# Sixteen heads of a batch in one PSUM bank, and the maxima turned in the other

## The reference

```
sc = silu(c); shift = sc @ shift_w.T + shift_b
scale = clip(sc @ scale_w.T + scale_b + 1, 0.1, 10)
adaln(x) = x / max(rms(x), 1e-6) * norm_w * scale + shift
q, k, v = heads of adaln(x) @ qkv_w.T
p = softmax(where(mask, q k^T / sqrt(8), -inf))
x = x + (p v) @ proj_w.T + proj_b
h1, h2 = split(adaln(x) @ w1.T + b1)
out = x + silu(h1) * h2 @ w2.T + b2
```

## Time and profile before

| | us |
|---|---|
| median of 3 runs | 184.35 |
| lowest, highest | 181.88, 184.48 |
| profiled execution, whole | 180.74 |
| its span in the profile | 178.8 |
| busy: PE, DVE, ACT, POOL | 146.9, 141.4, 134.7, 83.1 |

### The profile page before, as it was taken

One profiled execution on the slowest core, in us unless ns is written; L12 is line 12 of the kernel. 1 busy time (PEld: TensorE's weight loads), 2 busy tenths in 40 slices (PEclk: granted clock), 3 DMA queues, 4 the chain that ended last, 5 costly groups with the idle time before them and its releaser, 6 DMA issues.

```text
span 178.8 us, 3725 instructions
## 1 busy us (share of the span) xinstructions
PE 146.9 (82%) x1312; PEld 75.7 (42%) x1312; DVE 141.4 (79%) x248; ACT 134.7 (75%) x245; POOL 83.1 (46%) x133
## 2 busy tenths in 40 slices
PE   7778776668898889879769879788889976998992
PEld 7564233413333333333233333332225854785870
DVE  8756895978999999977999977996253947987992
ACT  8469862195897888958879958899877799599550
POOL 8319508965923304734618733335200525544650
PEclk9879999999999999999999999999999999999999
DMA  4847461537403375422022122022140300010103
GB/s 111 253 161 208 137 168 42 149 84 205 127 15 108 108 210 149 150 89 92 2 89 70 32 95 83 6 90 91 43 126 8 109 12 0 2 59 0 59 4 117
DMA packets 17512, 16.38 MB, mean 92 GB/s; under 512 B 2846, under 2 KB 16598, under 8 KB 17494
## 3 DMA queue, kind: packets, MB, share of 16 engines
q1 hardware_dynamic: 16086, 15.21, 27.6%
q0 software_dynamic: 1408, 0.93, 2.0%
HBM read 4.34 MB, written 5.24 MB: 54 GB/s over the span
## 4 chain that ended last, share of the span: by engine, by line
DVE 35%; PE 29%; issue 15%; ACT 10%; POOL 8%; DMA 2%; DVEq 0%; POOLq 0%; ACTq 0%
DVE neg_max L1107 24%; ACT p_exp L959 5%; POOL gated_lo L509 5%; PE bank L679 5%; PE bank L609 5%; PE bank L661 2%; DMA q_stack<-max_rows 2%; PE bank L635 2%; PE bank L630 2%; PE bank L564 2%; PE bank L728 2%; PE bank L529 1%; PE bank L553 1%; DVE rest L1082 1%; DVE k_stack L1017 1%
## 5 line engine op out<-in xcount | busy, mean ns | idle before, releaser
L1107 DVE TENSOR_REDUCE neg_max<-bank 128x2 f32<-128x512 f32 x128 | 81.5, 686 | 9.2 <-PE bank L609 8.8
L959 ACT ACTIVATE p_exp<-bank 128x512 f32<-128x512 f32 x128 | 69.8, 603 | 15.7 <-PE bank L661 14.6
L679 PE MATMUL bank<-p_exp,v_all 128*9 128x256 f32 x512 | 39.5, 381 | 0.3
L609 PE MATMUL bank<-k_stack,q_stack 62*128 62x256 bf16 x256 | 25.2, 271 | 17.2 <-DVE neg_max L1107 14.0
L509 POOL TENSOR_TENSOR gated_lo<-rs,gated_hi 128x512 fp32r<-128x512 f32 x14 | 18.2, 1302 | 28.8 <-ACT gated_hi L981 27.6
L473 POOL DMA_DIRECT2D q_stack<-max_rows x32 | 17.7, 556 | 22.7 <-DVE max_rows L1116 22.7
L661 PE MATMUL bank<-q_stack,k_stack 64*128 64x256 bf16 x256 | 25.3, 270 | 3.6 <-ACT p_exp L959 3.0
L609 PEld LDWEIGHTS bank<-k_stack,q_stack 62*128 62x128 bf16 x256 | 8.9, 93 | 43.4 <-DVE neg_max L1107 38.7
L463 POOL CAST max_parts<-neg_max 128x16 bf16<-128x16 f32 x16 | 3.1, 195 | 29.5 <-DVE neg_max L1107 29.5
L661 PEld LDWEIGHTS bank<-q_stack,k_stack 64*128 64x128 bf16 x256 | 12.2, 94 | 10.3 <-ACT p_exp L959 4.8
L728 PE MATMUL bank<-h_hi,w_parts 128*128 128x512 f32 x32 | 13.0, 407 | 1.6 <-DVE rs L1233 1.4
(11 more groups left out here) (115 smaller groups left out, 217.5 us busy)
## 6 DMA issues: line engine op xcount, KB each, us to landing
o_rows<-o_sb SPq DMA_DIRECT2D x16, 256.0 KB, 2.1
q_stack<-parts SPq DMA_DIRECT2D x18, 128.0 KB
k_stack<-parts SPq DMA_DIRECT2D x18, 128.0 KB
o_num<-o_rows SPq DMA_DIRECT2D x8, 128.0 KB, 2.4
o_den<-o_rows SPq DMA_DIRECT2D x8, 128.0 KB, 3.2
out_t<-o_num SPq DMA_DIRECT2D x8, 128.0 KB, 2.0
back<-back_w SPq DMA_DIRECT2D x1, 832.0 KB, 8.2
x_sb<-x_t SPq DMA_DIRECT2D x3, 256.0 KB, 4.9
```

Source lines behind the costliest of these rows:

```text
L609: mm = nc.tensor.matmul(scores[r][:, t * N:(t + 1) * N], q_stack[rows, c % STACKS, g, at + t * 128:at + (t + 1) * 128], k_stack[rows, c % ...
L679: mm = nc.tensor.matmul(bank[32 * j:32 * j + VW, 6 + k % 2, (q % 2) * N:(q % 2 + 1) * N], v_all[:, b, t, 2 * g + j, :], p_exp[:, (2 * q + ...
L959: nc.scalar.activation(p_exp[:, u % 4, par, :, :], bank[:, RING + v % RING, :].rearrange("p (t q) -> p t q", t=KT), ACT.Exp, scale=D ** -0 ...
L1107: nc.vector.tensor_reduce(out=neg_max[:, k % 2, :, par, g], in_=bank[:, n % RING, :].rearrange("p (t k) -> p t k", t=KT), axis=AX.X, op=AL ...
```

## The change

**One bank to a batch.** All 16 heads of a batch go into one bank, 6 for even batches and 7 for odd. Four quads of heads: quads 0 and 1 on rows 32j to 32j+8 (left and right half), quads 2 and 3 on rows 32j+16 to 32j+24. For that every head's piece of `v_all` is 25 columns wide, 8 values, a one and 16 zeros, and every stationary has 25 columns: for quads 0 and 1 it begins at the head's values, for quads 2 and 3 16 columns earlier, in the zeros of the head before. Quads add up in the bank; only the batch's first matmuls start it. ACT drains a bank once per batch (batches 0 to 5), DVE batches 6 and 7; one store and two loads per batch. `proj_w`'s rows are put in the new order on the host.

**Turns in the idle bank.** From k = 2 on the turned maxima go into bank 6 or 7, whichever the next batch will use, and no longer into the ring; they have semaphores of their own (`s_turn`, `s_turned`). The mean squares of chunks 0 and 1 go into bank 6 (`s_squares`). The first P times V of a batch waits for the copy of the second turn in its bank, the even turns wait for the drain of the batch before last.

**Constants.** POOL fills 16 zeros behind each head's one; `valid` shares memory with the mask to make room.

```diff
 RING = 3
+RING_TURNS = 2
...
-        items += [("turn", k) for k in range(HALVES) if turn_position(k) == p]
+        items += [("turn", k) for k in range(RING_TURNS) if turn_position(k) == p]
         items += [("project", c) for c in range(NC - 1) if project_position(c) == p]
-        items += [("square", c) for c in range(NC - 1) if square_position(c) == p]
+        items += [("square", c) for c in range(EARLY, NC - 1) if square_position(c) == p]
...
+def turn_bank(k):
+
+    return 6 + k // 2 % 2
+
+
+def square_bank(c):
+
+    return 6 + (BC * (c + 1)) % 2
...
-        v_all = sb("v_all", [C, B, KT, H, VW])
+        v_all = sb("v_all", [C, B, KT, H, V_WINDOW])
...
-            nc.gpsimd.memset(v_all[:, :, :, :, D:VW], 1.0).then_inc(s_const, 1)
+            heads = v_all.rearrange("p b t h w -> p (b t h) w")
+            nc.gpsimd.memset(heads[:, :, D:VW], 1.0).then_inc(s_const, 1)
+            nc.gpsimd.memset(heads[:, :, VW:V_WINDOW], 0.0).then_inc(s_const, 1)
...
             def turn_maxima(k):
-                turned = ring_bank(item("turn", k))
+                if k < RING_TURNS:
+                    turned, done = ring_bank(item("turn", k)), s_a
+                else:
+                    turned, done = bank[:, turn_bank(k), :], s_turn
+                    if k % 2 == 0 and k >= 4:
+                        pe.wait_ge(s_od, k // 2 - 1)
+                    if k % 2:
+                        pe.wait_ge(s_turned, k - RING_TURNS)
+                    for c in range(EARLY):
+                        if k == 4 * (c + 1) + 5:
+                            pe.wait_ge(s_inv2, 2 * c + 1)
                 pe.wait_ge(s_mp, 2 * (k + 1))
...
             def mean_square_2(c):
-                squares = ring_bank(item("square", c))
+                if c < EARLY:
+                    squares, done = bank[:, square_bank(c), :], s_squares
+                    pe.wait_ge(s_turned, 4 * (c + 1) + 4 - RING_TURNS + 1)
+                else:
+                    squares, done = ring_bank(item("square", c)), s_a
...
-                b, g = divmod(2 * q, G)
-                k = q // 2
+                b, quad = divmod(q, 4)
+                side, half = divmod(quad, 2)
                 if t == 0:
                     pe.wait_ge(s_e, 4 * q + 4)
...
-                    if q % 2 == 0 and k >= 2:
-                        pe.wait_ge(s_od, k - 1)
+                    if quad == 0 and b >= 1:
+                        pe.wait_ge(s_turned, 2 * b + 1 - RING_TURNS + 1)
                 for j in range(4):
-                    mm = nc.tensor.matmul(bank[32 * j:32 * j + VW, 6 + k % 2, (q % 2) * N:(q % 2 + 1) * N],
-                                          v_all[:, b, t, 2 * g + j, :],
+                    first = (4 * quad + j) * V_WINDOW - side * V_AT
+                    mm = nc.tensor.matmul(bank[32 * j:32 * j + V_WINDOW, 6 + b % 2, half * N:(half + 1) * N],
+                                          v_all[:, b, t, :, :].rearrange("p h w -> p (h w)")[:, first:first + V_WINDOW],
                                           p_exp[:, (2 * q + j // 2) % 4, j % 2, t, :],
-                                          start=(t == 0), stop=(t == KT - 1), tile_position=(0, 32 * j))
+                                          start=(quad == 0 and t == 0), stop=(quad == 3 and t == KT - 1),
+                                          tile_position=(0, 32 * j))
...
-                if u % 4 == 2 and 6 <= u < UNITS - 2:
-                    drain_output(u // 4 - 1)
+                if u % G == LAG and G < u < G * (B - 1):
+                    drain_output(u // G - 1)
...
-                if p == UNITS - 2 + LEAD:
-                    drain_output(HALVES - 2)
+                if p == G * (B - 1) + LAG + LEAD:
+                    drain_output(B - 2)
```

More of the change, by code:

```diff
@@ L26 @@
 VW = D + 1
+V_AT = 16
+V_WINDOW = V_AT + VW
 EPS = 1e-6
@@ L141, in drained @@
 def drained(n):
-    return sum(not (what[0] == "square" and what[1] < EARLY) for what in ITEMS[:n + 1])
+    return n + 1
+def turn_bank(k):
+    return 6 + k // 2 % 2
+def square_bank(c):
+    return 6 + (BC * (c + 1)) % 2
 def build(nc, x_t, small, mask, front_w, back_w, out_t):
-    o_rows = nc.dram_tensor("o_rows", [B, H, 32, N], F32).ap()
+    o_rows = nc.dram_tensor("o_rows", [B, 2, 4, 32, N], F32).ap()
     ctx = ExitStack()
@@ L378, in _ @@
                     stacks_of(e, j)
-            for k in range(HALVES):
-                if k == 3:
+            for b in range(B):
+                if b == BC - 1:
                     stacks_of(NP - 1, 0)
[L382 to L385, removed]
+                store_outputs(b)
+                load_outputs(b)
+                if b == BC - 1:
                     stacks_of(NP - 1, 1)
@@ L466, in _ @@
                                         ALU.subtract).then_inc(s_mp, 1)
-                pool.wait_ge(s_ad, drained(item("turn", k)))
+                pool.wait_ge(*((s_ad, drained(item("turn", k))) if k < RING_TURNS else (s_turned, k - RING_TURNS + 1)))
                 c, at = divmod(k // 2, BC)
@@ L586, in ring_bank @@
                 if n >= RING:
-                    if ITEMS[n - RING][0] == "square" and ITEMS[n - RING][1] < EARLY:
-                        pe.wait_ge(s_inv2, 2 * ITEMS[n - RING][1] + 1)
-                    else:
-                        pe.wait_ge(s_ad, drained(n - RING))
+                    pe.wait_ge(s_ad, drained(n - RING))
                 return bank[:, n % RING, :]
@@ L632, in mean_square_2 @@
             def mean_square_2(c):
[L633 removed]
+                if c < EARLY:
[3 more added lines that the diff above has]
+                    squares, done = ring_bank(item("square", c)), s_a
                 pe.wait_ge(s_sq2, c + 1)
[L635 removed]
+                nc.tensor.matmul(squares, mean_w[:, :], sq2[:, c % 2, :], start=True, stop=True).then_inc(done, 1)
             def zero_outputs():
@@ L920, in square_2 @@
                 act.wait_ge(s_y3, 1)
-                act.wait_ge(s_a, item("square", c - 2) + 1)
+                act.wait_ge(s_squares, c - 2 + 1)
                 nc.scalar.activation(sq2[:, c % 2, :], y[:, c, :], ACT.Square).then_inc(s_sq2, 1)
@@ L925, in ln_norm_2 @@
                 if c < EARLY:
-                    n = item("square", c)
-                    act.wait_ge(s_a, n + 1)
-                    nc.scalar.activation(rs2[:, c, :], bank[:, n % RING, :], ACT.Ln, bias=words[:, 2:3]).then_inc(s_inv2, 1)
+                    act.wait_ge(s_squares, c + 1)
+                    nc.scalar.activation(rs2[:, c, :], bank[:, square_bank(c), :], ACT.Ln,
+                                         bias=words[:, 2:3]).then_inc(s_inv2, 1)
                     return
@@ L1263, in turned @@
         return np.ascontiguousarray(np.asarray(a).T)
+    by_output = [(m % 2) * C // 2 + (m // 2) * D + d for m in range(H) for d in range(D)]
     by_row = [(2 * g + r) * D + d for r in range(2) for d in range(D) for g in range(G)]
```

67 lines of the change are left out of this document (36 added, 31 removed).

## The result

| | before | changed |
|---|---|---|
| median, us (20 runs each) | 183.8 | 186.11 |
| lowest | 181.0 | 184.1 |
| profiled execution, whole | 180.74 | 188.29 |
| its span | 178.8 | 186.5 |

The ratio is 1.0192, with a 95% interval of 1.0154 to 1.0229: slower, by about 2%. The forecast of 180.6 us was wrong in sign, and 186.11 lies outside its range.

What follows compares the result with a forecast made beforehand. The prediction took the middle as bound by DVE's maxima waiting for PE's scores behind turned maxima in the three-bank ring. It summed 3.9 - 0.3 - 0.4 + 0.47 - 0.3 = 3.4 us gained, forecasting 180.6 us, range 177.0 to 183.6.

Steps and rivals of the forecast that it cites:

- the zeros in `v_all`: At the start: POOL's extra memset takes 3.6 us while POOL is idle, costing nothing; upper bound 2.1 us.
- rival 4: At the start: POOL's zeros come late by up to 2.1 us; 1.3 gained, 183.1 us. Chance 0.08.
- The turns, 9 x 0.43: Middle: turned maxima out of the ring save 0.43 us at k = 4-7, 9-11, 13, 14; 3.9 us together.
- Turns 2, 3, 8 and 12: Middle: k = 3 is late anyway; 2 waits for the maxima's DMA, 8 and 12 for POOL's square; 0 gained.
- rival 1: Middle: the DMA of the turned maxima becomes the bound; 1.5 us gained, 182.8 us. Chance 0.20.
- The 0.3 taken off for k = 4: At k = 4: the turn can't come sooner, so it gives 0.12 us, not 0.43; minus 0.3.
- The wider loads: P times V: 25 columns instead of 9 cost 0.04 us a group; 0.4 on the turns' path, 0.3 in the tail.
- rival 3: PE becomes the bound through loads at 0.11 us a group; 0.9 us lost, 185.3 us. Chance 0.10.
- The tail, +0.47 for a copy of ACT: From 120 us on: one drain per batch removes ACT's copy at 122.03 from the deciding path; 0.47 us gained.

Runs made afterwards that it cites:

- e2: The kernel before, with only v_all widened to 25 columns and its zeros set at the start; stationaries stay at 9 columns. 186.89 us, ratio 1.0195.
- e9: The changed kernel with half of the zeros set at the start and the other half behind the first K stacks. 185.88 us, ratio 1.0183.
- e5: Second run of e1's kernel: the changed kernel with POOL's memset of the zeros moved behind the first K stacks' DMAs. 181.43 us, ratio 0.993.
- e10: e8 with POOL's last three pieces of work on w_parts moved from turns 9, 10, 11 to 11, 12, 13. 180.11 us, ratio 0.9821.
- e12: e10 with POOL's six subtractions at k = 6, 7, 8, 10, 11, 12, none at 9 or 13. 177.9 us, ratio 0.9709.
- e7: The kernel before with the ones of v_all set behind the first stacks and ten unread float32 matmuls at position 6. 182.59 us, ratio 0.9982.
- e4: The kernel before with 25-column stationaries, v_all wide and its zeros set late. 182.76 us, ratio 1.0089.
- e6: e5 with ten unread float32 matmuls in PE's 2.60 us of idle time at position 6. 180.56 us, ratio 0.989.
- e11: e3 with the ones of v_all set late too and ten unread matmuls at position 6. 180.27 us, ratio 0.9874.
- e3: e1 with turns and mean squares back in the ring of three banks; one drain per batch and 25 columns stay. 183.6 us, ratio 0.9962.
- e8: The changed kernel with zeros and ones of v_all set behind the first stacks and ten unread matmuls at position 6. 180.82 us, ratio 0.9839.
- e1: The changed kernel with POOL's memset of the zeros moved behind the first K stacks' DMAs. 183.14 us, ratio 1.0059.

## Why the prediction was wrong

**The step that failed** is the one on the zeros in `v_all`: "POOL is idle until 12.58 (6.64 us), so nothing". The size was right (3.6 us forecast, 3.70 measured) and POOL was idle; but only who waits for POOL was asked, not who shares something with it while it runs. Cost: a stall 4.20 us longer (0.85 to 5.05), 3.8 to 4.8 us at the first maximum, ratio 1.0195 alone (e2). The range for it, 0 to 2.1 through late K stacks, had the wrong mechanism, and rival 4 the right place for the wrong reason. The trace of before had the sign: 0.85 us for an operation on 128x8 whose neighbours take 0.2, beside the ones' memset. The Trainium skill (SBUF — State Buffer, Who interferes with whom) has the rule: `tensor_scalar` on DVE can enter a mode that takes the port pair shared with GpSimd, whoever issues first holds it for its whole instruction and the other blocks fully. This trace agrees in that the DVE instruction ends with POOL's (9.51 and 9.48 us, in e9 7.74 and 7.72). It does not agree on who is first: DVE's record starts at 4.46, those of the two memsets of `v_all` at 5.37 and 5.78, and DVE loses. Why, no run here shows. That memset and stall go together is shown by the series; that the shared port is the reason is the skill's account, which no run here tested by itself.

**The turns, 9 x 0.43.** The mechanism was right, and the size for four of the nine. In e5 turns 4, 5, 6 and 13 gave 0.45, 0.48, 0.46 and 0.47, turns 10, 11 and 14 less, 0.32, 0.28 and 0.25: 2.7 us together. In the changed kernel itself it is 2.1: turns 4 to 6 gave 1.10 in place of 1.39, and turn 10 nothing. Turns 2, 3, 8 and 12 gave nothing, as forecast. Two of the nine lost instead:
- *Turn 7.* ACT's logarithm of the sums waits for their load back from HBM: 0.65 us in the changed kernel, 0.35 in e5, 0.71 in e10, 1.07 in e12, none in before's profile. The stretch k = 7 to 8 is 7.32, 7.03, 7.39 and 7.76, in each case 6.67 to 6.69 plus that wait (6.86 before). So the turn gave 0.18 and the wait took more. But the wait is not shown to be the change's doing: e7, with before's turns and drains, has it too, 1.11 us, and its stretch is 7.98, 6.87 plus the wait. The changed kernel, e12 and e7:

```profile
78.17 0.63 ACT L847 ACTIVATE o_den<-o_den 128x512 f32<-128x512 f32 x1 [0.65 <-DMA o_den<-o_rows]
```

```profile
71.82 0.63 ACT L854 ACTIVATE o_den<-o_den 128x512 f32<-128x512 f32 x1 [1.07 <-DMA o_den<-o_rows]
```

```profile
71.71 0.63 ACT L824 ACTIVATE o_den<-o_den 128x512 f32<-128x512 f32 x1 [1.11 <-DMA o_den<-o_rows]
```

- *Turn 9.* The collision with POOL's subtraction. The normalisation is 0.45 longer (1.70 to 2.15), which takes the gain. In e5 the clock is low behind it, from 90.9 us, and the stretch is 0.99 longer than before. e4, with before's turns and a normalisation of 1.70, is 0.99 longer too, with the clock low from 92.4: that part is the clock's.

**Turn 4 and rival 1.** The 0.3 taken off for k = 4 was right in some executions and not in others. Rival 1 (the DMA of the maxima as bound) held in the period of this turn. Where PE waits for that DMA, the period is longer: no wait and 5.22 us in e5, 0.33 us of wait (at 67.02) and 5.34 in the changed kernel, 0.51 and 5.53 in e6. So turn 4 gave 0.45, 0.33 and 0.14 of its 0.43.

**The wider loads** (0.4 and 0.3 taken off). One load went from 88 to 102 ns, the 14 forecast; the group of P times V from 0.62 to 0.63 us, and the units did not change (e4 against before). By the traces the 0.7 us should have been 0 and rival 3 was wrong; e4's time leaves it open, as said.

**The tail, +0.47 for a copy of ACT.** e11 shows 0.09 from the last copy to the end and 0.07 in the stretch before. The term was mis-sized: 0.16 where 0.47 was forecast. Which wait takes the rest stays open.

**The clock** had no term in the sum, and it decides how much of the turns' gain reaches the time. A low stretch of 3.4 us goes with 1.2 to 1.9 us: k = 0 to 1 is 9.89 without one, 11.37 to 11.54 with one (e6, e4), 12.67 to 12.90 with 6.8 us of it, and k = 6 to 7 is 7.53 with one in e3, 5.68 without. Behind its first maximum before's profile has none until the end; e5 has three (from 26.1, 32.9 and 90.9 us), which take back more than its turns gave.

In time the turns' gain is therefore not shown. Of e5's executions those with a granted clock of 0.971 to 0.972 have a median of 180.6 us (6), those of before in the same series at 0.970 to 0.972 183.4 (14). But these 14 lie from 181.92 to 185.32, and against the lower six the difference is 1.6 us and not 2.8; up to 1.25 of it can be PE's faster start. e8 against e7 (ratios 0.9839 and 0.9982) points to a gain; but where the turns alone are put back, e8 (180.82) and e11 (180.27) can't be told apart, nor e5 and e3.

It may be that kernels with shorter units are granted the low level more often: the medians of the granted clock are 0.954 to 0.971 for the changed kernel, e5, e6, e8, e10 and e12 (e1 0.953, e9 0.944), all with turns out of the ring, and 0.972 to 0.99 for before (0.972 to 0.981 in four series), e2, e3, e4, e7 and e11. The series are small and lie on different chips. Whether shorter periods bring the low clock on, or the idle places that they leave, stays open.

Forecast: 3.4 us gained. Measured: 2.3 lost by the medians. Without the zeros at the start the two medians lie 0.2 us above and 2.0 us under before's (e1, e5), though the traces show 2.7 us off the units.

## What to carry to other kernels

A filler on an idle engine is not free by that alone: ask also which engine works beside it. Look in the trace for an instruction far longer than its neighbours of the same size, since such a stall was shown here as busy time on the engine that was held. Put a large memset beside work that it was seen not to hold (as in e5, below), not beside a chain of small operations that everything hangs on. When a stretch gets shorter, list what runs beside it at a fixed place (another engine's work, a DMA), since each can take back its part. And before a difference between two profiles is laid to an edit, compare the places that the edit does not touch: here the start alone differed by 1.2 us between kernels that were the same there.

## What the runs showed of the hardware

- A POOL memset of 128x4096 float32 in runs of 16 (3.70 us) held a DVE `tensor_scalar` of 128x8, in and out of SBUF, until its end: 0.24, 0.85, 3.28, 5.05 us by the amount of `v_all` memset beside it.
- The same memset moved to 19.23 us held nothing of DVE's that ran beside it; e5's timeline, POOL and DVE:

```profile
18.91 2.53 DVE L1137 TENSOR_REDUCE neg_max<-bank 128x2 f32<-128x512 f32 x4
19.23 3.68 POOL L472 MEMSET v_all<- 128x4096 f32 x1
...
21.36 0.68 DVE L1102 TENSOR_TENSOR rest<-bank,parts 128x512 f32<-128x512 f32 x1
21.96 0.68 DVE L1094 SCALAR_TENSOR_TENSOR xn<-rs,x_sb 128x512 f32<-128x512 f32 x1
```

The last of these has two inputs in SBUF and takes 0.68 us, as it does at 18.31 ahead of the memset. The normalisation, of the same kind, takes 0.67 alone and 1.70 or 2.15 beside a POOL subtraction that reads SBUF. The Trainium skill (SBUF — State Buffer, Who interferes with whom) draws that line: two SBUF inputs contend with a GpSimd instruction that reads SBUF, not with one that only writes. These rows agree. One row has no explanation here: the `xn` operation of the same kind took 1.20 us at 15.04 in e5 (and at 16.24 before), while POOL was issuing the DMAs of the first K stacks.
- Four column tiles of 25 columns, two quads to a bank at rows 0 and 16 of a tile, cost PE 14 ns more a load and made no unit of the trace longer (e4 for the columns, e11 with two quads as well).
